# Attention's small products behind the maxima: one reordered step order in a fused five-stage kernel

## What is computed

```python
dots = jnp.einsum('bhid,bhjd->bhij', q, k) * SCALE
m = jax.nn.softmax(dots, axis=-1)
diag = jnp.diagonal(m, axis1=-2, axis2=-1)
mu = diag.mean(axis=-1, keepdims=True)
sd = diag.std(axis=-1, ddof=1, keepdims=True)
keep = jnp.abs((diag - mu) / sd) <= Z_THRESH
valid = keep[..., :, None] & keep[..., None, :]
masked = jnp.where(valid, dots, NEG)
attn = jax.nn.softmax(masked, axis=-1)
row_any = jnp.any(valid, axis=-1, keepdims=True)
attn = jnp.where(row_any, attn, 0.0)
out = jnp.einsum('bhij,bhjd->bhid', attn, v)
```

## Time and the profile before

| what | value |
|---|---|
| median of three runs | 2108.51 us (2108.24 to 2112.3) |
| the profiled execution, its own time | 2106.37 us |
| its span, first to last instruction | 2105.1 us |
| granted TensorE clock, mean | 0.958 |
| busy share of PE, DVE, ACT, POOL | 90%, 63%, 53%, 56% |
| first T product to the last S product of attention | about 869 to 1882 us |

### The profile page before, as it was taken

How to read it: one execution, slowest core, us unless ns; L and a number is a source line. 1 busy time by engine, 2 the same in 40 slices (tenths; PEclk the granted TensorE clock), 3 DMA queues, 4 the chain that set the end, 5 groups by cost and what they waited for, 6 DMA issues and landing times. The chain is left out here.

```text
span 2105.1 us, 22037 instructions
## 1 busy us (share of the span) xinstructions
PE 1888.8 (90%) x7432; PEld 1316.8 (63%) x7432; DVE 1332.4 (63%) x2215; ACT 1124.6 (53%) x1586; POOL 1177.1 (56%) x645
## 2 busy tenths in 40 slices
PE   5996787876997965899999999999999999998588
PEld 3772343333775643677777777777777777775366
DVE  5426888896336761666666666666666757665376
ACT  4327667553425453565555556555565656553344
POOL 2440657663454552266666575766666656668454
PEclk8998999999998996999999999999999999999799
DMA  2000000000001004213131313131313131300100
GB/s 90 0 1 1 0 0 1 0 1 0 0 1 45 1 23 95 59 42 74 38 74 37 74 38 74 37 74 37 74 38 74 37 74 39 69 11 11 50 5 16
DMA packets 46049, 74.53 MB, mean 35 GB/s; under 512 B 26864, under 2 KB 28528, under 8 KB 45680
## 3 DMA queue, kind: packets, MB, share of 16 engines
q1 hardware_dynamic: 43744, 72.35, 14.8%
q10 hardware_dynamic: 2160, 0.77, 0.1%
q0 software_dynamic: 32, 0.00, 0.0%
HBM read 20.93 MB, written 1.18 MB: 11 GB/s over the span
## 5 line engine op out<-in xcount | busy, mean ns | idle before, releaser
L1993 POOL TENSOR_TENSOR at_e_lo<-at_e,at_e_hi 128x1024 fp32r<-128x1024 f32 x256 | 613.9, 2398 | 396.6 <-DVE at_e_hi L1966 395.0
L1821 ACT ACTIVATE at_e<-at_ps 128x1024 f32<-128x1024 f32 x256 | 263.0, 1027 | 315.4 <-PE at_ps L1728 315.4
L1813 ACT ACTIVATE at_ps<-at_ps,at_neg_diag 128x1024 f32<-128x1024 f32 x256 | 278.6, 1088 | 115.9 <-DVE at_neg_diag L1881 115.9
L1888 DVE TENSOR_REDUCE at_row_max<-at_ps 128x1 f32<-128x1024 f32 x256 | 311.2, 1215 | 15.6 <-PE at_ps L1707 12.5
L1881 DVE CUSTOM_DVE_ANT_0 at_junk_diag<-at_ps,ident 128x128 bf16<-128x128 f32 x256 | 74.5, 291 | 322.0 <-PE at_ps L1680 321.9
L1966 DVE CAST at_e_hi<-at_e 128x1024 fp32r<-128x1024 f32 x256 | 220.3, 860 | 30.3 <-ACT at_e L1821 29.7
L920 POOL TENSOR_TENSOR mb_work<-mb_work,mb_c 128x1024 f32<-128x1024 f32 x64 | 151.9, 2373 | 145.4 <-DVE mb_work L894 144.6
L386 POOL TENSOR_TENSOR ffn_lo<-ffn_hid,ffn_hi 128x512 fp32r<-128x512 f32 x96 | 124.4, 1297 | 180.8 <-DVE ffn_hi L313 180.8
L1678 PE MATMUL at_ps<-at_k,at_q 128*128 128x512 f32 x512 | 172.2, 418 | 16.5 <-DMA at_k<-at_qk_lo 14.1
L1707 PE MATMUL at_ps<-at_k,at_q 128*128 128x512 f32 x512 | 173.9, 421 | 12.2 <-DMA at_k<-at_mask_rows 9.8
L1747 PE MATMUL at_pv_ps<-at_e_lo,at_v_hi 128*128 128x512 f32 x512 | 161.4, 396 | 8.2 <-POOL at_e_lo L1993 8.2
(11 more groups left out here) (315 smaller groups left out, 3803.4 us busy)
## 6 DMA issues: line engine op xcount, KB each, us to landing
at_q<-at_qk_hi SPq DMA_DIRECT2D x64, 256.0 KB, 3.7
at_k<-at_qk_hi SPq DMA_DIRECT2D x32, 512.0 KB, 5.9
at_q<-at_qk_lo SPq DMA_DIRECT2D x32, 256.0 KB, 6.4
at_k<-at_qk_lo SPq DMA_DIRECT2D x32, 256.0 KB, 6.2
at_recips<-at_recip_row SPq DMA_DIRECT2D x32, 256.0 KB, 3.5
ffn_h_raw<-in_h SPq DMA_DIRECT2D x2, 1024.0 KB, 8.7
at_head_w_raw<-in_w_qkv SPq DMA_DIRECT2D x32, 64.0 KB, 4.2
x<-in_x SPq DMA_DIRECT2D x4, 256.0 KB, 5.0
```

The source lines that it names most:

```text
L1813: act.eng.activation(ps[:], ps[:], ACT.Exp, scale=SCALE, bias=m.small["neg_diag"][s][:, blk:blk + 1], accum_out=m.small["sums"][s][:, blk: ...
L1821: act.eng.activation(m.e[e % 2][:], slot("turned_scores", h, blk)[:], ACT.Exp, scale=SCALE).then_inc(sem["at_exp"])
L1888: dve.eng.tensor_reduce(m.small["row_max"][h % SLOTS][:, blk:blk + 1], slot("best", h, blk)[:], AX.X, ALU.max).then_inc(sem["at_best_out"])
L1993: pool.eng.tensor_tensor(m.e_lo[e % 3][:], m.e[e % 2][:], m.e_hi[e % 3][:].bitcast(F32), ALU.subtract).then_inc(sem["at_lo"])
```

## The change

The small products go behind B in TensorE's step and in the order of slots, and `best` goes ahead of the small work on VectorE. Everything from B on moves one step later (AT_BEST 12 to 13, AT_SHIFT, AT_TURNED, AT_PV and what follows, each by one), queries and keys one step earlier (AT_QK -7 to -8, AT_SPLIT -10 to -11). The mask stays at 11. The values are due two steps ahead of their first use instead of three. SH becomes one transpose, of `row_max`; `shift_rows` adds the mask rows on VectorE. SyncE issues the mask rows ahead of the reciprocals' spread, as both now fall into phase 3. Phases after: QK 0, M 1, SQ 2, MK 3, SH 5, split 5, norm 5, W's result copied 0, reciprocals 2, V 6 and 2, OUT 7.

```diff
@@ -1392,15 +1392,15 @@
 
 
 
-AT_FIRST, AT_LAST = -BLK * 2, BLK * (NH - 1) + BLK * 5
+AT_FIRST, AT_LAST = -BLK * 2, BLK * (NH - 1) + BLK * 5 + 1
 STATS = 7
 SHIFT_ROW, MASK_ROW = 0, 32
 CROSS, MAIN = 0, 1
 PARTS = 7
 
 
-AT_SPLIT, AT_QK, AT_SCORES, AT_STATS, AT_MEAN, AT_SQUARE, AT_MASK, AT_BEST, AT_SHIFT = -10, -7, 0, 8, 9, 10, 11, 12, 20
-AT_TURNED, AT_PV, AT_PV_OUT, AT_RECIP, AT_SPREAD, AT_NORM, AT_OUT = 22, 23, 31, 33, 34, 36, 38
+AT_SPLIT, AT_QK, AT_SCORES, AT_STATS, AT_MEAN, AT_SQUARE, AT_MASK, AT_BEST, AT_SHIFT = -11, -8, 0, 8, 9, 10, 11, 13, 21
+AT_TURNED, AT_PV, AT_PV_OUT, AT_RECIP, AT_SPREAD, AT_NORM, AT_OUT = 23, 24, 32, 34, 35, 37, 39
 
 
 def due(t, offset, n=1):
@@ -1413,7 +1413,7 @@
 
     for g in range(NH // GROUP):
         for part in range(2):
-            if t == AT_PV + g * GROUP * BLK + part * (BLK // 2) - 3:
+            if t == AT_PV + g * GROUP * BLK + part * (BLK // 2) - 2:
                 return g, part
     return None
 
@@ -1429,18 +1429,18 @@
     for t in range(AT_FIRST, AT_LAST):
         if at := due(t, AT_TURNED, BLK):
             order.append(("turned_scores", *at))
+        if at := due(t, AT_SCORES, BLK):
+            order.append(("scores", *at))
+        if at := due(t, AT_BEST, BLK):
+            order.append(("best", *at))
         if at := due(t, AT_MEAN):
             order.append(("mean", *at))
         if at := due(t, AT_SQUARE):
             order.append(("square", *at))
         if at := due(t, AT_MASK):
             order.append(("turn_mask", *at))
-        if at := due(t, AT_SCORES, BLK):
-            order.append(("scores", *at))
         if at := due(t, AT_SHIFT):
             order.append(("turn_shift", *at))
-        if at := due(t, AT_BEST, BLK):
-            order.append(("best", *at))
         if at := due(t, AT_QK):
             order.append(("qk", *at))
         if at := group_due(t):
@@ -1623,10 +1623,10 @@
     for t in range(AT_FIRST, AT_LAST):
         if at := due(t, AT_PV_OUT):
             move_den(at[0])
+        if at := due(t, AT_MASK):
+            move_mask(at[0])
         if at := due(t, AT_SPREAD):
             spread_recip(at[0])
-        if at := due(t, AT_MASK):
-            move_mask(at[0])
         if at := due(t, AT_SHIFT):
             move_shift(at[0])
         if at := due(t, AT_RECIP):
@@ -1711,10 +1711,8 @@
     def turn_shift(h):
         pe.wait_ge(sem["at_best_out"], h * BLK + BLK)
         slot_free(pe, c, m, "turn_shift", h)
-        turned = slot("turn_shift", h)[0:BLK, 0:P]
-        pe.eng.matmul(turned, m.small["dropped"][h % SLOTS][:], c.ident[:], start=True, stop=False)
-        pe.eng.matmul(turned, m.small["row_max"][h % SLOTS][:], c.ident[:],
-                      start=False, stop=True).then_inc(sem["at_turn_shift"])
+        pe.eng.transpose(slot("turn_shift", h)[0:BLK, 0:P], m.small["row_max"][h % SLOTS][:],
+                         c.ident[:]).then_inc(sem["at_turn_shift"])
 
     def turned_scores(h, blk):
         q, k = m.Q[h % SLOTS], m.K[h % SLOTS]
@@ -1762,18 +1760,18 @@
     for t in range(AT_FIRST, AT_LAST):
         if at := due(t, AT_TURNED, BLK):
             turned_scores(*at)
+        if at := due(t, AT_SCORES, BLK):
+            scores(*at)
+        if at := due(t, AT_BEST, BLK):
+            best(*at)
         if at := due(t, AT_MEAN):
             mean(at[0])
         if at := due(t, AT_SQUARE):
             square(at[0])
         if at := due(t, AT_MASK):
             turn_mask(at[0])
-        if at := due(t, AT_SCORES, BLK):
-            scores(*at)
         if at := due(t, AT_SHIFT):
             turn_shift(at[0])
-        if at := due(t, AT_BEST, BLK):
-            best(*at)
         if at := due(t, AT_QK):
             project(at[0])
         if at := group_due(t):
@@ -1917,13 +1915,16 @@
         dve.wait_ge(sem["at_turn_mask"], h + 1)
         if h >= 2:
             dve.wait_ge(sem[f"mask_move{h % 2}"], 16 * (h // 2))
+            dve.wait_ge(sem["at_shift"], h - 2 + 1)
         dve.eng.tensor_copy(m.mask_rows[h % 2][:], slot("turn_mask", h)[0:BLK, 0:P]).then_inc(sem["at_mask"])
 
     def shift_rows(h):
         dve.wait_ge(sem["at_turn_shift"], h + 1)
+        dve.wait_ge(sem["at_mask"], h + 1)
         if h >= 2:
             dve.wait_ge(sem[f"shift_move{h % 2}"], 16 * (h // 2))
-        dve.eng.tensor_copy(m.shift_rows[h % 2][:], slot("turn_shift", h)[0:BLK, 0:P]).then_inc(sem["at_shift"])
+        dve.eng.tensor_tensor(m.shift_rows[h % 2][:], slot("turn_shift", h)[0:BLK, 0:P], m.mask_rows[h % 2][:].bitcast(F32),
+                              ALU.add).then_inc(sem["at_shift"])
 
     dve.wait_ge(sem["attn_load"], 2 * 16)
     dve.wait_ge(sem["attn_out_load"], 16)
@@ -1952,22 +1953,22 @@
             diagonal(*at)
         if at := due(t, AT_STATS):
             first_stats(at[0])
+        if at := due(t, AT_TURNED, BLK):
+            e = at[0] * BLK + at[1]
+            dve.wait_ge(sem["at_exp"], e + 1)
+            if e >= 3:
+                dve.wait_ge(sem["at_pv"], e - 3 + 1)
+            dve.eng.tensor_copy(m.e_hi[e % 3][:], m.e[e % 2][:]).then_inc(sem["at_hi"])
+        if at := due(t, AT_BEST, BLK):
+            best(*at)
         if at := due(t, AT_MEAN):
             negate_mean(at[0])
         if at := due(t, AT_SQUARE):
             keeps(at[0])
         if at := due(t, AT_MASK):
             mask_rows(at[0])
-        if at := due(t, AT_TURNED, BLK):
-            e = at[0] * BLK + at[1]
-            dve.wait_ge(sem["at_exp"], e + 1)
-            if e >= 3:
-                dve.wait_ge(sem["at_pv"], e - 3 + 1)
-            dve.eng.tensor_copy(m.e_hi[e % 3][:], m.e[e % 2][:]).then_inc(sem["at_hi"])
         if at := due(t, AT_SHIFT):
             shift_rows(at[0])
-        if at := due(t, AT_BEST, BLK):
-            best(*at)
     dve.wait_ge(sem["x_attn"], NH // 2)
```

## The result

The changed kernel takes 2080.23 us (median of four runs, 2076.49 to 2083.6) against 2109.72 for the kernel before (2108.24 to 2112.3): a ratio of 0.9861, interval 0.9849 to 0.9873, so 1.4% faster. Its profiled execution is the slowest of its four, 2083.6 us, and that of before the fastest of its own, 2106.37; between the two traces lie 22.8 us of the 29.5 between the medians.

The account below looks back on a forecast made before the run. TensorE's step bounds full steps (busy 1009.15 of 1013.00 us). Full steps 12.3 plus start 6 less end 0.5 is 17.8 off 2106.37, giving 2088.6; plus 2.1 for the median, 2091 us; own range 2083 to 2099.

Parts of the forecast that it names:

- the whole range: Total time of the kernel: 2073 to 2106 us, wider than the forecast's own range.
- The chain through the norm: GpSimd and VectorE, phases 5 to 7: B of phase 7 stalls 0.7 us without V in phase 6, 0.4 with.
- The rival that the chain does not bind: VectorE or GpSimd have more slack, so the 0.7 and 0.4 stalls go: 17.5 us more saved, 2073; chance 0.15.
- The small products: TensorE: M, SQ, MK behind B and SH as one transpose together save 1.20 us a head.
- One price of 0.27 for all: TensorE: each small product behind B costs 0.25 us plus 0.02 for the exponential's gate.
- The estimate that the prediction set beside its row: Skill's load price on TensorE: M and SQ 0.21 us, transposes about 0.11; total some 8 us lower, 2083.
- The small products as dear as before: TensorE: the exponential's gate follows them behind B, only SH saves 0.26 us; total 2112; chance 0.15.
- The negated mean late: VectorE: held until GpSimd is done, exponential 0.9 us late; 26.6 more, 2117; chance 0.10, with any other late link.
- The keeps: VectorE, at T+4.3 beside GpSimd's `at_e_lo`: about 1.4 us each, still in time for the mask.
- V behind SQ: TensorE: a group's second V waits 1.2 us for S's slot instead of 0.65, 0.55 more once in four heads.
- The sum: Full steps: four heads save 1.75 us, seven groups 12.3; with start and end 17.8 in all.
- Start and end: Attention's start gains 6 us, near the middle of bounds 0 and 13.2; its end loses 0.5.

Follow-up runs that it names:

- Experiment 1: Changed kernel with SH done twice, as plain products with the identity instead of one transpose: 2081.97 us (ratio 0.9869 to the kernel before).
- 2: Changed kernel with GpSimd's weight split one step earlier (AT_SPLIT -11 to -12): 2074.74 us (ratio 0.9836 to the kernel before).
- 3: Changed kernel with most of the norm left out, 32 of 1024 columns from the third head on: 2059.07 us (ratio 0.9761).
- 10: Changed kernel, all work kept, with the norm in phase 0, OUT in phase 4 and two buffers for weighed values: 2072.31 us (ratio 0.9825).
- experiment 4: Changed kernel with small products ahead again (SH between S and B) and VectorE's order as before: 2093.03 us (ratio 0.9919).
- experiment 9: Changed kernel with MK and SH as plain products with the identity instead of transposes: 2089.63 us (ratio 0.991).
- experiment 6: Changed kernel with queries, keys and weight split back by one step (AT_QK -7, AT_SPLIT -10): 2116.71 us (ratio 1.0038).
- 5: Kernel before with only the order changed: small products behind B, maximum first on VectorE, no step moved, SH a pair: 2141.15 us (ratio 1.0158).
- 7: Changed kernel with queries, keys and split back by one step, but QK right behind B, ahead of M: 2103.5 us (ratio 0.9972).
- experiment 8: Changed kernel with the values V issued right behind B, ahead of SQ: 2074.0 us (ratio 0.983).

## Why the prediction was right, and where its numbers were not

It forecast 2091 us; 2080.23 came, inside the whole range, and below the forecast's own (2083 to 2099). The mechanism was the forecast one. The sum was too small by a third and more, 17.8 us where attention gained 28.2 in the traces: small products, stall, V and start all came out better than forecast, and only the end worse.

- **The chain through the norm.** Right in place and price: 0.7 in phase 7 of a head without V, and 0.40 of wait by name; 0.35 after V where 0.4 was said. With OUT it is 0.6. Experiment 1 added work ahead of the chain and the stall shrank by it; 2, 3 and 10 moved one of its links, and the stall followed. The rival that the chain does not bind is refuted.
- **The small products.** One price of 0.27 for all was the step that was mis-sized. Measured behind B: M and SQ 0.32, MK and SH 0.13. SQ saved 0.15 (0.21 said), M with QK 0.20 (0.27), MK 0.36 (0.23), SH 0.63 (0.49): 1.34 a head for 1.20. Behind the error is a misreading of the earlier trace rows: I took MK's 0.25 for "its two passes" and a restart, where the row says x1. SH's saving can't be split into fixed shares for place and form. As a pair of products it costs 0.74 behind B (experiment 1) and 0.76 between S and B, so the place alone gives nothing; as one transpose it costs 0.55 between S and B (experiment 4) and 0.13 behind B. Behind B the second product is worth 0.2 and the form 0.4 (experiment 9). The estimate that the prediction set beside its row, from the Trainium skill's page "TensorE: Matmul & The Clock Gate", section "LDWEIGHTS (loading the stationary operand)", gave 0.11 for the transposes, nearer to the 0.13 measured than my 0.27. That is luck in part: it counted two passes, where the rows have one. It would also give the plain product with the same 8 columns 0.11, where 0.5 was measured, and its 0.21 for M and SQ is further from 0.32 than my 0.27. The same page's section "Terms" has: loads and products of trn2 gained a transpose mode, four times faster for FP32. The 0.5 against 0.13 here is of that size, but the 0.5 holds gaps as well as passes.
- **The small products as dear as before** was refuted by experiment 4: the place (with VectorE's order) is worth 0.16 to 0.42 each.
- **The negated mean late** was refuted by the trace: it took 0.15 us under GpSimd's work. What reads PSUM was not held and what reads SBUF was; the rule of the Trainium skill's page "SBUF — State Buffer", section "Who interferes with whom", by which an instruction of VectorE in a two-port mode, which a tensor_scalar can enter, is blocked while GpSimd holds the shared ports, agrees with the second. The keeps took 1.13 us (1.4 said), and nothing in full steps waited for them. VectorE's rows of tile `at_keep` (duration minimum, median, maximum; the two waits lie at the start):

```profile
L1909 DVE TENSOR_SCALAR at_keep<-at_dev,at_limit,at_varies x32: 291/1131/1134, 831.2 to 1866.2; 128x8 f32<-128x8 f32 x32
...
who waited for it (us, times):
  PEld at_ps L1698: 1.6, 2
  PE at_ps L1698: 0.8, 1
```

- **V behind SQ** cost 0.44 per four heads (0.55 said).
- **The sum.** In full steps four heads gained 2.8, not 1.75, and 28 heads 21.0 us (the first four a little more than the rest), not 12.3. Per four heads the difference is 0.56 from the small products, 0.3 from a smaller stall (2.2 us, where 2.5 was said) and 0.1 from V.
- **Start and end.** Timed from attention's first product, the first T came 8.8 us sooner (79.3 to 70.5, experiment 6) where 6 was said. That 6 was a middle between bounds and not a size worked out; the reason given, the phases that the parts of Q and K gain against the maxima, is borne out in part: the waits for mask rows at the start are 9.8 us with none gained, 5.4 with one (experiment 6) and 2.6 with two. What else shortened the start was not separated. The end of attention lost 1.6 us, not 0.5: the last four heads took 113.5 us instead of 111.9, and the last OUT came no later after them. Start, full steps and end are 28.2 us in the traces, close to the 29.5 of the medians. The 22.8 between the two traces are fewer because that of the changed kernel is 3.7 us longer ahead of attention and 1.8 behind it, in stages that the change doesn't touch.

What the prediction did not see is what the moved steps are for. It costed queries and keys in phase 0 and never asked what they would cost in phase 1 behind M. Experiments 5 to 7 answer. The order alone loses 32 us, and without the step for queries and keys the whole change is slower than before: QK then stands behind M in the ring, and SyncE's transfers of the parts delay the mask rows.

## What to carry to other kernels

When items share a small ring of buffers, an item's price is read from the reader of the item that many places before it, so adding or moving a small product reprices the next three; write the ring's order down for every phase before costing a move. A stall behind a chain through a slower engine is a floor: work added ahead of it is nearly free (2.1 of 2.4 us in four heads here) and work saved ahead of it is lost, until a link of the chain is moved to a step that is long for another reason. A gain in one step is checked in the next one too, for half of it can stand there (experiment 8). A gain at the start of a stage is timed from the stage's first instruction, since two executions can reach it 4 us apart.

## What the hardware showed that was not expected

- The same 8x128 turn costs TensorE 0.13 us as a transpose (one pass) and 0.5 as an f32 product with the identity (two passes, and gaps on both sides).
- VectorE's cast ended 0.55 us after the GpSimd operation that it waited for, in each place shown here (0.56 once), whether it took 2.62 us in all or 1.44. The keeps, between SBUF tiles, took 1.13 us instead of 0.29; the limit, read from PSUM, took 0.15.
